# Placing the lower products of a graph layer by the room in each slot of a Mamba scan, on one Trainium2 core

## What is computed

```
h = relu(layernorm(x));  x = x + relu(adj_norm @ h @ W.T + b)       # layer 0, adj_norm: scaled by degrees
h = relu(layernorm(x));  x = x + mamba(ln(relu(adj @ h @ gcn_w + gcn_b)))   # layer 1
mamba: xz = h @ w_in;  u = silu(conv4(xz[:, :256]) + conv_b);  dbc = u @ w_xp
       dt = softplus(dbc[:, :8] @ w_dt + b_dt);  B, C = the 16 + 16 other columns of dbc
       state = exp(dt * A) * state + dt * B * u          (one step per node, 256 x 16 states)
       y = (state @ C + u * D) * silu(z);  out = y @ w_out
```

## Time and profile before

| | |
|---|---|
| median of 3 runs | 2652.01 us (2651.05 to 2652.62) |
| the profiled execution | 2651.2 us, its span 2649.4 us |
| TensorE busy | 2247.8 us (85%) |
| VectorE busy | 2075.0 us (78%) |
| GpSimd busy | 1067.5 us (40%) |
| ScalarE busy | 978.7 us (37%) |
| HBM read | 625.28 MB |

### The profile page before, as it was taken

The page is one execution under the profiler, slowest core; times in us unless marked ns, Lnnn a source line. Parts: engine busy times, 40 slices in busy tenths (PEclk is TensorE's granted clock), DMA queues, the critical chain, the costliest instruction groups (busy, mean ns, idle before and its releaser), DMA issues.

```text
span 2649.4 us, 21934 instructions
## 1 busy us (share of the span) xinstructions
PE 2247.8 (85%) x6864; PEld 1276.2 (48%) x6864; DVE 2075.0 (78%) x2079; ACT 978.7 (37%) x1696; POOL 1067.5 (40%) x461
## 2 busy tenths in 40 slices
PE   0237688999999999999999988888888888886776
PEld 0113344444447888888886434444444443443333
DVE  5898888886645666565653399999999999999997
ACT  0000000000004555554552355555555555555552
POOL 0000000000000000000000299999999999999554
PEclk9978789999999999999999999998999999997888
DMA  8999999998766666555546656665665665662221
GB/s 336 379 395 410 394 393 386 367 410 330 264 266 239 214 221 214 196 211 196 200 175 235 251 208 224 203 218 203 223 217 191 215 218 204 207 225 69 72 72 52
DMA packets 108323, 643.00 MB, mean 243 GB/s; under 512 B 14224, under 2 KB 15024, under 8 KB 42672
## 3 DMA queue, kind: packets, MB, share of 16 engines
q1 hardware_dynamic: 92160, 604.02, 60.8%
q10 hardware_dynamic: 16048, 37.57, 4.0%
HBM read 625.28 MB, written 16.25 MB: 242 GB/s over the span
## 4 chain that ended last, share of the span: by engine, by line
PE 55%; DVE 29%; issue 7%; ACT 4%; DMA 1%; ACTq 1%; DVEq 0%; POOL 0%; SPq 0%; POOLq 0%
PE ps L830 21%; PE ps L748 13%; DVE arena L563 11%; PE ps L870 10%; DVE ps L666 6%; DVE arena L681 5%; PE ps L948 4%; DVE ring L681 3%; PE ps L770 2%; PE ps L899 2%; ACTq L978 1%; DMA diag_h<-adj 1%; PE ps L910 1%; PE ps L891 1%; PE ps L929 1%
## 5 line engine op out<-in xcount | busy, mean ns | idle before, releaser
L451 POOL TENSOR_TENSOR rstd<-base,minus_half 128x8 f32<-128x8 f32 (+1 forms) x40 | 84.7, 2118 | 1445.2 <-DVE base L503 876.0
L830 PE MATMUL ps<-adj_parts,h_parts 128*128 128x512 f32 x2592 | 593.6, 390 | 2.5 <-ACT adj_parts L1044 2.1
L870 PE MATMUL ps<-ring,diag_h 128*128 128x512 f32 x1152 | 564.6, 625 | 0.9 <-DVE arena L653 0.9
L830 PEld LDWEIGHTS ps<-adj_parts,h_parts 128*128 128x128 f32 x2592 | 484.7, 188 | 108.8 <-ACT adj_parts L1044 4.6
L563 DVE TENSOR_TENSOR arena<-arena,ring 128x2048 f32<-128x2048 f32 x208 | 476.8, 2292 | 65.2 <-DMA ring<-adj 47.4
L748 PE MATMUL ps<-ring,arena 128*128 128x512 f32 x928 | 433.4, 628 | 62.4 <-DMA ring<-adj 62.2
L681 DVE TENSOR_TENSOR_SCAN arena<-arena,state,ps 128x512 f32<-128x512 f32 x312 | 382.4, 1267 | 29.2 <-ACT arena L1119 8.9
L467 POOL TENSOR_TENSOR arena<-arena 128x1024 f32<-128x1024 f32 x156 | 377.6, 2431 | 67.9 <-ACT state L1111 67.8
L870 PEld LDWEIGHTS ps<-ring,diag_h 128*128 128x128 f32 x1152 | 229.1, 201 | 253.9 <-issue 248.7
L1119 ACT ACTIVATE arena<-arena,a_sb 128x512 f32<-128x512 f32 x512 | 338.4, 708 | 0.4
L590 DVE TENSOR_TENSOR adj_parts<-ring,adj_parts 128x1024 fp32r<-128x1024 f32 x216 | 264.0, 1224 | 94.4 <-ACT adj_parts L1044 83.5
(11 more groups left out here) (93 smaller groups left out, 1974.0 us busy)
## 6 DMA issues: line engine op xcount, KB each, us to landing
ring<-adj SPq DMA_DIRECT2D x480, 1024.0 KB, 6.6
arena<-c_scratch SPq DMA_DIRECT2D x128, 512.0 KB, 4.2
diag_h<-adj SPq DMA_DIRECT2D x32, 1024.0 KB, 12.1
arena<-x ACTq DMA_DIRECT2D x16, 512.0 KB, 5.0
x_scratch<-arena ACTq DMA_DIRECT2D x8, 512.0 KB, 3.0
arena<-x_scratch ACTq DMA_DIRECT2D x16, 256.0 KB, 5.5
out<-arena ACTq DMA_DIRECT2D x16, 256.0 KB, 4.1
lower_scratch<-arena ACTq DMA_DIRECT2D x7, 512.0 KB, 2.6
```

What stands on the lines that cost most here:

```text
L830: last = nc.tensor.matmul(acc[:, c, :], h_parts[:, blk % 2, layer, h_part, a * F:(a + 1) * F], adj_parts[:, buf, adj_part, c * MM:(c + 1) ...
L870: last = nc.tensor.matmul((acc_c if i else y_ps)[:, c, :], tile_of(h1, JT * s + a), blk[:, a * STRIP + c * MM:a * STRIP + (c + 1) * MM], s ...
```

## The change

A function counts the units of small products that TensorE has in a slot (a unit is as long as one lower product), and the lower products of strips 1 to 7 go where a slot holds fewer than LEVEL = 4 units, in proportion to that room. Over the slots -19 to 204 the room is 576 units for 544 products. The handover follows the strip's last product, but not before `earliest`, three slots after the GCN stage whose input buffer it overwrites. The DT stages and the pick are not counted.

```diff
+LEVEL = 4
+
...
+def small_products(g):
+
+    units = 0
+    for stage, count in ((GCN, 1), (TRANSPOSE, 1), (XZ, CONV), (XZ + 1, CONV), (XZ + 2, 1), (XZ + 3, 1), (DBC, 2),
+                         (OUT, 2), (QSUM, 2), (QSUM + 4, 2), (QSUM + 8, 2), (QSUM + 12, 2)):
+        units += count * (chunk_at(g, stage) is not None)
+    return units
...
     start, end = FIRST_SLOT, DS * CPS * (NS - 1) + GCN
     total, n = sum(len(m) for m in mms[1:]), 0
+    room = list(itertools.accumulate(max(LEVEL - small_products(g), 0) for g in range(start, end)))
+
+    def slot_for(n):
+
+        return min(start + sum(r <= n * room[-1] // total for r in room), end)
+
     for i in range(1, NS):
         for mm in mms[i]:
-            products[max(start + n * (end - start) // total, handover[i - 1])].append(mm)
+            products[max(min(slot_for(n), end - 1), handover[i - 1])].append(mm)
             n += 1
-        handover[i] = min(start + n * (end - start) // total + 1, end)
+        earliest = DS * (CPS * (i - 1) - 1) + GCN + 3 if i >= 2 else start
+        handover[i] = min(max(slot_for(n) + 1, earliest), end)
```

More of the change, by code:

```diff
@@ L19 @@
+import itertools
 from contextlib import ExitStack
```

## The result

The changed kernel takes 2668.0 us (median, 2667.11 to 2669.91) beside 2652.3 us for the kernel before (median of 4): a ratio of 1.0058, 95% interval 1.0046 to 1.0070, so 15.7 us or 0.6% slower. The forecast was 2668.4 us, slower. The profiled execution took 2669.91 us, its span is 2668.1 us.

A forecast was written before the change was run, and what follows sets the result against it. TensorE was taken to bound the lead-in and VectorE the scans. 11.5 + 1.0 + 7.0 + 3.0 - 7.1 + 1.0 = +16.4 us on 2651.2 gave 2667.6, with 0.8 for the median 2668.4; range 2656 to 2677.

The forecast's parts named there:

- Lead-in: Slots -19 to -2, ahead of scan 0: ten more products cost 8.6 us and uncovered waits 2.9, together 11.5 us.
- Handover 2: Slot 2: the handover waits for TensorE's end of strip 2 and for its second input, costing 1.0 us.
- Pile of 13: Slot 32: 13 products behind the handover make scan 34 wait, 4.3 us at full rate, about 7.0 with half-rate clock.
- Pile of 9: Slot 64: nine products behind the handover cost 0.9 us at full rate, 3.6 with half rate; taken as 3.0.
- Slots 6 to 9: In each chunk, with no products in the XZ slots, the pick and output matmul waits go: a gain of 7.1 us.
- Scan 15: Slots 14 and 15 of each chunk: paired waits for pick and ScalarE mostly absorb extra products, costing 1.0 us.
- The clock was not kept up: Rival: levelled products keep TensorE's full rate, waits in slots 14 and 15 vanish too, 2636.5 us, faster; chance 0.05.
- The loads were not late: Rival: block loads in the scans come late, about 1 us more in each of 13 chunks, 2681 us; chance 0.04.
- The costs did not meet at their lower ends: Rival: piles at full rate, lead-in waits covered, slots 14 and 15 giving back, about 2656 us, no change; chance 0.12.

The follow-up runs named there:

- spread_piles: The changed kernel with strips 3 to 7 laid out by room within their own slots, so without the piles of 13 and 9: 2659.3 us, ratio 1.0024.
- old_lead_in: The kernel before with its 44 lead-in products and handovers kept, products laid by room within each strip's slots only from slot -1 on: 2647.2 us, ratio 0.9980.
- old_lead_in_13: As old_lead_in, but with no product in slot 13 of any chunk, its products going to the other slots: 2647.6 us, ratio 0.9973.
- late_24: Against old_lead_in, 22 products instead of 44 in slots -19 to -2, the others moved into the scans by a per-slot table, no piles: 2628.5 us, ratio 0.9906.

## Why the prediction was right, point by point

**Lead-in (11.5 us predicted, 12.1 measured).** The mechanism is shown from both sides: 54, 44, 32 and 22 products give 66.2, 54.1, 44.8 and 38.6 us whatever lies behind them. The 0.6 us missing are the three restarts of TensorE after a wait, less the one that the kernel before had.

**Handover 2 (1.0, measured 1.47).** As argued.

**Pile of 13 (7.0; a wait of 5.49, a delay of 6.8).** The time from the handover's start to scan 34's multiply was forecast as 9.1 + 7.0 = 16.1 us and is 1673.11 - 1657.17 = 15.9, so against the 9.1 of the kernel before scan 34 comes 6.8 us later. TensorE's side was right, half rate included. What the prediction missed is that VectorE's pace is no longer 9.1 us after the change: it is 10.4 even without the pile (spread_piles, from 1657.44 to 1667.84), as `nmr` takes 1.9 us there. Behind the pile this hides under the wait, which is shorter for it.

**Pile of 9 (3.0; a wait of 2.00, a delay of 3.4).** The same: from the handover at 1807.46 to scan 66 at 1819.92 are 12.5 us, where the prediction had 9.1 + 3.0 = 12.1. The half rate itself came later than the prediction has it: the clock was still at 1.00 when TensorE's wait for the handover began, and fell within it.

**Slots 6 to 9 (-7.1).** All eleven waits went, 7.1 us; old_lead_in shows the same gain without the rest.

**Scan 15 (+1.0).** The pairs went from 22.2 to 23.7 us, +1.5. The prediction counts eight slots 13 whose products change and overlooks slot 29, which goes from two to none. That the pick's waits there are covered by ScalarE was argued from one row; old_lead_in_13 showed it.

**Sum.** The waits alone give 12.1 + 1.5 + 5.5 + 2.0 - 7.1 + 1.5 = 15.5 us, and the two long `nmr` 2.6 more: 18.1. Measured from the first handover addition to scan 205's multiply it is 12.1 + 5.9 = 18.0 us in the profile of the changed kernel, and 18.4 in that of its second series. The forecast has 16.4 for the same terms, so it is 1.6 us short: 0.6 in the lead-in, 0.5 each in handover 2 and scan 15, and nothing much in the piles. That the medians differ by only 15.7 us, and the forecast's 2668.4 so meets the measured 2668.0, is luck: the interval of the ratio allows 12 to 19 us, the phases ahead vary by 6, and the time from the last multiply to the end is 16.3 us in seven of the profiles (the changed kernel's) and 17.5 to 17.9 in four (17.7 in the kernel before).

**The rivals.** The clock was not kept up: it is 0.95 in the scans before and after, and waits of up to 2.69 us still stand ahead of scan 15. The loads were not late: TensorE waits for no transfer in the scans, before or after, and the ring's loads land there in 6.5 us (median), where it was 6.4 before. The costs did not meet at their lower ends either: the waits of the lead-in were exposed and the piles entered at half rate.

## What to carry to other kernels

Filler work is only free where the engine that does it isn't the one that sets the end: look at each stage by itself before work is spread by one rule over all. Here one product cost 0.6 to 1.2 us ahead of the first scan, with the waits that it covers or uncovers, and next to nothing in the scans. So the same 22 products were worth some 16 us by their place (38.6 + 904.0 us in late_24, 54.1 + 904.6 in old_lead_in); and where a cut-off (here the earliest handover) holds work back, spread it between the cut-offs, or it piles up behind one, on a TensorE that has had too little work to hold its clock. Before an engine's waits are removed, ask who would be late next: 14.3 us of waits went in old_lead_in_13 and the time didn't move.

## What the runs showed of the hardware

**A VectorE instruction of 4 columns that takes 1.9 us.** `nmr` took as long as GpSimd's instruction still had to run, in the changed kernel:

```profile
1665.73 1.90 DVE L526 SCALAR_TENSOR_TENSOR nmr<-mv,rstd 128x4 f32<-128x4 f32 x1
```

```profile
1665.26 2.34 POOL L486 TENSOR_TENSOR arena<-arena 128x1024 f32<-128x1024 f32 x1
```

It ends at 1667.63, GpSimd's multiply at 1667.60. In the kernel before it ended with GpSimd's addition (2.34 us from 1648.42), and took less, as less of that was left:

```profile
1650.18 0.59 DVE L507 SCALAR_TENSOR_TENSOR nmr<-mv,rstd 128x4 f32<-128x4 f32 x1
```

It took 0.14 us at 1510.33, when GpSimd was idle. The Trainium skill (SBUF — State Buffer, section on who interferes with whom) says that VectorE and GpSimd share a pair of ports under an exclusive lock, which an instruction of VectorE with two inputs in SBUF needs while GpSimd reads SBUF; the rows agree for `nmr`, whose inputs both lie there. The multiply and the additions with an input in PSUM keep their 1.2 us under the same GpSimd work. GpSimd is busy 865 of 915 us of the scans. A handover in slot 16, 32 or 64 puts `nmr` of the next slot some 0.46 us behind the start of a GpSimd instruction of 2.35 us: it takes 1.9 us in the next slot in every profile with such a handover (after one in slot 33 it took 1.77 in that same slot), and 0.6 in the others. Moving the handover changed by 1.3 us what a 0.14 us instruction costs.

**The phases ahead vary by 6 us** between profiles whose programs are the same up to there, and by 1.5 us between the two of the changed kernel. Differences of a few us in the scan stage are read from the first handover addition on, better than from the whole.
